# Row maxima issued from ScalarE's queue, group pair sums on GpSimd, and gate products in front of the first maxima

## The reference

```python
q = (q_input @ Wq.T + bq).reshape(B, T, N_HEADS, HEAD_DIM)   # 16 heads of 16
k = q_input @ Wk.T + bk                                      # one head, shared
v = q_input @ Wv.T + bv
mask = pos[None, :] < pos[:, None]                           # strictly causal
attn = softmax(where(mask, einsum('bhtd,bsd->bhts', q, k) * scale, -1e30))
out = einsum('bhts,bsd->bhtd', attn, v) @ Wo.T + bo
...
scores = sigmoid(xf @ w_router); sfc = scores + corr_bias    # 32 experts
top2, _ = top_k(sfc.reshape(T, 8, 4), 2)
group_scores = top2.sum(-1)                                  # best 4 of 8 groups
combine = top 6 experts of these groups, weighted by scores
eo = (silu(x @ gate_w[e]) * (x @ up_w[e])) @ down_w[e]
result = x + attention + sum(combine * eo) + shared expert (width 352)
```

## Time and profile before

| | us |
|---|---|
| median of 3 runs | 699.68 |
| lowest and highest | 697.82, 701.73 |
| profiled execution, its own time | 701.01 |
| profiled execution, span of the trace | 699.2 |

### The profile page before, as it was taken

How to read it: one execution, slowest core, us unless ns; L and a number is a source line. 1 busy time by engine, 2 the same in 40 slices (tenths; PEclk the granted TensorE clock), 3 DMA queues, 4 the chain that set the end, 5 groups by cost and what they waited for, 6 DMA issues and landing times.

```text
span 699.2 us, 13166 instructions
## 1 busy us (share of the span) xinstructions
PE 598.8 (86%) x4249; PEld 334.7 (48%) x4250; DVE 380.7 (54%) x1156; ACT 290.7 (42%) x649; POOL 305.2 (44%) x258
## 2 busy tenths in 40 slices
PE   5959698895879679878969999999999999999940
PEld 2424243442545345534535555555555555555540
DVE  6516874893554355521116656655666665665436
ACT  3644223433332333344454554554454554454400
POOL 4120212130344644465613566566556556556610
PEclk9979899999898889988999999999999999999975
DMA  9679947499587973258754666666666666666479
GB/s 306 164 144 203 351 170 262 61 272 366 161 256 225 318 254 112 101 171 312 277 184 77 105 114 106 106 109 111 105 108 112 104 110 111 105 108 94 55 270 352
DMA packets 73907, 122.92 MB, mean 176 GB/s; under 512 B 12208, under 2 KB 57456, under 8 KB 73328
## 3 DMA queue, kind: packets, MB, share of 16 engines
q1 hardware_dynamic: 50112, 85.22, 41.2%
q0 software_dynamic: 20736, 29.05, 24.3%
q10 hardware_dynamic: 2992, 7.80, 3.1%
HBM read 61.41 MB, written 62.52 MB: 177 GB/s over the span
## 4 chain that ended last, share of the span: by engine, by line
PE 71%; DVE 10%; issue 7%; DMA 7%; SPq 3%; ACT 1%; another core or an unknown queue 1%; POOL 0%; ACTq 0%; DVEq 0%; POOLq 0%
PE bank L1536 20%; PE bank L1562 13%; PE bank L1473 5%; DVE mx L938 5%; PE bank L1518 4%; PE bank L1410 4%; PE bank L1366 4%; PE bank L1392 4%; PE bank L1551 3%; PE bank L1481 2%; PE bank L1369 2%; PE bank L1339 2%; DMA weights<-q_d 2%; SPq L586 2%; PE bank L1394 2%
## 5 line engine op out<-in xcount | busy, mean ns | idle before, releaser
L1306 POOL DMA_INDIRECT acc_d<-attT,xnT x112 | 176.6, 1577 | 146.9 <-ACT attT L821 114.5
L938 DVE TENSOR_REDUCE mx<-bank 128x1 f32<-128x384 f32 (+7 forms) x154 | 106.0, 710 | 80.2 <-PE bank L1369 70.4
L1536 PE MATMUL bank<-weights,xnT 128*64 x448 | 144.5, 465 | 2.6 <-DVE attT L1102 2.4
L1265 POOL DMA_INDIRECT xg_d<-stage,posu x96 | 92.6, 965 | 111.5 <-PE bank L1410 89.7
L766 ACT ACTIVATE xnT<-bank 128x1024 f32<-128x1024 f32 (+1 forms) x72 | 61.7, 882 | 112.8 <-PE bank L1394 76.4
L1562 PE MATMUL bank<-weights,xnT 88*64 x448 | 106.0, 379 | 0.5 <-issue 0.5
L1536 PEld LDWEIGHTS bank<-weights,xnT 128*64 128x64 f32 x448 | 56.7, 136 | 64.1 <-issue 62.4
L1562 PEld LDWEIGHTS bank<-weights,xnT 88*64 88x64 f32 x448 | 61.1, 136 | 41.8 <-issue 17.2
L1102 DVE COPY attT<-weights 128x704 f32 x56 | 29.5, 527 | 92.0 <-PE bank L1539 83.6
L1539 PE MATMUL bank<-attT,xnT 128*64 128x352 f32 x224 | 78.3, 472 | 0.0
L821 ACT ACTIVATE attT<-bank,xnT 128x256 f32<-128x256 f32 x112 | 53.2, 475 | 54.5 <-PE bank L1565 54.5
(11 more groups left out here) (152 smaller groups left out, 1059.5 us busy)
## 6 DMA issues: line engine op xcount, KB each, us to landing
weights<-in_wts SPq DMA_DIRECT2D x32, 608.0 KB
xg_d<-weights SPq DMA_DIRECT2D x28, 584.0 KB, 9.5
stage<-xg_d SPq DMA_DIRECT2D x56, 146.0 KB
xnT<-xg_d SPq DMA_DIRECT2D x56, 146.0 KB
acc_d<-weights SPq DMA_DIRECT2D x8, 512.0 KB, 9.2
q_d<-weights SPq DMA_DIRECT2D x8, 384.0 KB, 3.4
weights<-q_d SPq DMA_DIRECT2D x12, 256.0 KB, 8.6
weights<-q_d SPq DMA_DIRECT2D x48, 64.0 KB, 7.6
```

The costliest lines, as they stand in the source:

```text
L938: eng.tensor_reduce(mx[:, b % 2, h0:h0 + nh * pair, i].rearrange("p (k h) -> p k h", k=pair), bank[:, k:k + pair, 0:wide].rearrange("p k ( ...
L1265: eng.indirect_dma_start(out=xg_d[:, :], out_offset=bass.IndirectOffsetOnAxis(ap=posu[:, t, k:k + 1], axis=0), in_=stage[:, t % NST, :], i ...
L1306: eng.indirect_dma_start(out=acc_d[a][:, :], out_offset=bass.IndirectOffsetOnAxis(ap=index[:, i % NIX:i % NIX + 1], axis=0), in_=ys[y], in ...
L1536: eng.matmul(bank[0:SR, k, 0:2 * M], xgT[i % 4][:, c, 0:SR], weights[:, bass.ds(expert[i] * WCOL + c * 2 * M, 2 * M)], start=(c == 0), sto ...
```

## The change

- The five first products of batch 1 (gate 0, up 0, gate 1, up 1, gate 2, with two gating multiplications) come ahead of the first maxima; they were spread among them.
- The three transfers of a batch's maxima are issued by ScalarE, in a step of their own (`max_out`), no longer by SyncE in `mrows`.
- Maxima and clamp of batches 1 to 3 end at place 36 of 48, `mrows` comes at 38, `max_out` at 40. The rest of the routing is a stream of its own, over places 1 to 42 of batch 0.
- At the end of the opening, gate 0 and up 0 of batch 3 stand between `clamp` and `mrows`.
- The bias and the six pair sums go to POOL (`group_pairs`), into six buffers; VectorE takes the maximum of the six in one reduction (`group_max`).
- Scatters are split 2/5, 2/5 and 1/5 over batches 1 to 3 (they were 3/8, 3/8 and 1/4), the last part ends at place 28, no longer at 34; the first rows are loaded two places earlier.

```diff
-    early = proj_steps((2, KC), (3, KC)) + [("values", 2), ("values", 3), ("sigmoid",)] + gate_steps(1)[:3]
-    later = gate_steps(1)[3:] + proj_steps((2, 0), (2, 1)) + gate_steps(2) + proj_steps((3, 0), (3, 1))
+    steps += gate_steps(1)[:7]
+    early = proj_steps((2, KC), (3, KC)) + [("values", 2), ("values", 3), ("sigmoid",)]
+    later = gate_steps(1)[7:] + proj_steps((2, 0), (2, 1)) + gate_steps(2) + proj_steps((3, 0), (3, 1))
...
-    steps += [("clamp", 0), ("mrows", 0)] + gate_steps(3) + [("warm",)]
+    last = gate_steps(3)
+    steps += [("clamp", 0)] + last[:2] + [last[3], ("mrows", 0), last[2], ("max_out", 0)] + last[4:] + [("warm",)]
...
-    third = len(sends) * 3 // 8
+    third = len(sends) * 2 // 5
...
-        [(0, 40, merged(max_steps(1), routing[EARLY_ROUTING:]) + [("clamp", 1), ("mrows", 1)]),
+        [(0, 36, max_steps(1) + [("clamp", 1)]), (37, 38, [("mrows", 1)]), (39, 40, [("max_out", 1)]), (1, 42, routing[EARLY_ROUTING:]),
...
-        [(14, 26, [("down", 2, i) for i in range(IT)]), (0, 34, sends[2 * third:]), (1, 2, load_steps(*DIES[1])),
+        [(14, 26, [("down", 2, i) for i in range(IT)]), (0, 28, sends[2 * third:]), (1, 2, load_steps(*DIES[1])),
...
+            def group_pairs(n):
+                if n == 0:
+                    w.wait_ge(sigmoid_done, 1)
+                    w.wait_ge(proj_in, 16)
+                    w.wait_ge(pool_ready, 6)
+                    own.mark(eng.tensor_tensor(sfc[:, :, 0:E], scores, cb_sb.unsqueeze(1).to_broadcast([P, NT, E]), ALU.add))
+                    w.wait_ge(pool_step, own.n)
+                for i, (a, c) in enumerate((((0, 1), (0, 2)), ((0, 3), (1, 2)), ((1, 3), (2, 3)))[n]):
+                    eng.tensor_tensor(pairs[:, 2 * n + i], grp[:, :, :, a], grp[:, :, :, c], ALU.add).then_inc(pairs_ready, 1)
...
-                elif kind == "groups":
-                    group_scores(*a)
+                elif kind == "group_max":
+                    w.wait_ge(pairs_ready, 6)
+                    own.mark(eng.tensor_reduce(gsum[:, :, 0:G], pairs.rearrange("p k t g -> p t g k"), AX, ALU.max))
```

More of the change, by code:

```diff
@@ L64 @@
 NPAD = 4
-EARLY_ROUTING, EARLY_CLEARS = 9, 18
+EARLY_ROUTING, EARLY_CLEARS = 10, 18
 CLEARED = (NSLOT + NPAD - 1) // NPAD
@@ L241, in make_plan @@
                         [("zero", n) for n in range(2 * ZEROED)]))],
-        [(0, 40, max_steps(2) + [("clamp", 2), ("mrows", 2)]), (14, 46, [("down", 0, i) for i in range(IT)]),
-         (2, 48, sends[:third]), (8, 48, load_steps(0, DIES[0][0]))],
-        [(0, 40, max_steps(3) + [("clamp", 3), ("mrows", 3)]), (14, 40, [("down", 1, i) for i in range(IT)]),
+        [(0, 36, max_steps(2) + [("clamp", 2)]), (37, 38, [("mrows", 2)]), (39, 40, [("max_out", 2)]), (14, 46, [("down", 0, i) for i in range(IT)]),
+         (3, 48, sends[:third]), (8, 48, load_steps(0, DIES[0][0]))],
@@ L245, in make_plan @@
+        [(0, 36, max_steps(3) + [("clamp", 3)]), (37, 38, [("mrows", 3)]), (39, 40, [("max_out", 3)]), (14, 40, [("down", 1, i) for i in range(IT)]),
          (0, 48, sends[third:2 * third]), (43, 44, load_steps(*DIES[0]))],
-        [(14, 26, [("down", 2, i) for i in range(IT)]), (0, 34, sends[2 * third:]), (1, 2, load_steps(*DIES[1])),
+        [(14, 26, [("down", 2, i) for i in range(IT)]), (0, 28, sends[2 * third:]), (1, 2, load_steps(*DIES[1])),
          (14, 15, load_steps(*DIES[2])), (27, 28, load_steps(*DIES[3])), (35, 36, load_steps(*DIES[4])),
-         (16, 17, [("spread",)]), (20, 21, [("experts",)]), (40, 41, [("first_rows",)]), (46, 47, load_steps(*DIES[5]))],
+         (16, 17, [("spread",)]), (20, 21, [("experts",)]), (38, 39, [("first_rows",)]), (46, 47, load_steps(*DIES[5]))],
@@ L378, in build @@
         sfc = carve([NT, E + 2])
-        pairs = carve([2, NT, G])
+        pairs = carve([6, NT, G])
         gsum = carve([NT, G + 4])
@@ L587, in stack @@
                                   q_d[b, QP[r]].rearrange("(d h) t -> d h t", h=NH)[:, heads, :]).then_inc(stacked[b][g], 16)
-            def max_rows(b):
-                w.wait_ge(mpart_done, b + 1)
-                for j in range(3):
-                    eng.dma_start(qs[b % 2][96 + j:97 + j, :, :].rearrange("p h (i t) -> p (h i) t", t=P),
-                                  mpart[0:NH * IT, b % 2, j, :]).then_inc(max_in[b % 2], 16)
             def clear(n):
@@ L651, in sync_program @@
                     stack(*a)
-                elif kind == "mrows":
-                    max_rows(*a)
                 elif kind == "clear":
@@ L780, in turned_heads, with max_rows @@
                          bank[:, k, :].rearrange("p (i c t) -> p i c t", i=2, c=KC)).then_inc(emptied[k], 1)
+            def max_rows(b):
+                w.wait_ge(mpart_done, b + 1)
+                for j in range(3):
+                    eng.dma_start(qs[b % 2][96 + j:97 + j, :, :].rearrange("p h (i t) -> p (h i) t", t=P),
+                                  mpart[0:NH * IT, b % 2, j, :]).then_inc(max_in[b % 2], 16)
             def gate(b, c):
@@ L853, in scalar_program @@
                     gate(*a)
+                elif kind == "max_out":
+                    max_rows(*a)
                 elif kind == "sa":
@@ L978, in heads @@
                                   ALU.mult).then_inc(emptied[k], 1)
-            def group_scores(n):
-                if n == 0:
-                    w.wait_ge(sigmoid_done, 1)
-                    w.wait_ge(pool_ready, 5)
-                    own.mark(eng.tensor_tensor(sfc[:, :, 0:E], scores, cb_sb.unsqueeze(1).to_broadcast([P, NT, E]), ALU.add))
-                for a, c in (((0, 1), (0, 2)), ((0, 3), (1, 2)), ((1, 3), (2, 3)))[n]:
-                    dst = gsum[:, :, 0:G] if (a, c) == (0, 1) else pairs[:, 0]
-                    w.wait_ge(dve_step, own.n)
-                    own.mark(eng.tensor_tensor(dst, grp[:, :, :, a], grp[:, :, :, c], ALU.add))
-                    if (a, c) != (0, 1):
-                        w.wait_ge(dve_step, own.n)
-                        own.mark(eng.tensor_tensor(gsum[:, :, 0:G], gsum[:, :, 0:G], pairs[:, 0], ALU.max))
             def top(src, dst, done, quarter):
@@ L1280, in gpsimd_program @@
                     split_low(*a)
+                elif kind == "groups":
+                    group_pairs(*a)
                 elif kind == "rmask":
```

8 lines of the change are left out of this document (4 added, 4 removed).

## The result

| | before | after |
|---|---|---|
| median, us | 700.7 | 681.64 (4 runs) |
| lowest and highest, us | 697.82, 701.88 | 678.0, 683.76 |
| ratio to before, 95% interval | | 0.9728 [0.9671, 0.9786] |
| profiled execution, its own time / span | 701.01 / 699.2 | 683.21 / 681.1 |

The changed kernel is 19 us faster. The forecast said 29.3 us faster. The time lies inside the range, near its upper end, and 11 us above the point. In a later group of runs the same kernel came to 0.9664 [0.9610, 0.9719] of the kernel before, 24 us. The question for the experiments is therefore where 5 to 10 us of the forecast went.

A forecast was written before the change was run, and what follows sets the result against it. TensorE (PE), busy 86% of the span, was taken as the bound; only the start of the expert rounds could move. 18 + 4 + 5 + 2.3 + 0 = 29.3 us off the 699.68 median gave 670.4 us, range 660 to 683.

The forecast's parts named there:

- 8.7 + 3.0 - 1.4: Opening: five products leave the maxima stretch (8.7 us), half clock becomes full (3.0), maxima start 1.4 us later.
- two rivals: Opening stays DVE's: 679.4 us, chance 0.2. Maxima land no earlier at two boundaries: 681.7 us, chance 0.14.
- 12.3 us of 18: Whole opening, up to batch 0's first scores: forecast gain 18 us, bounds 9 and 21.7.
- the rival: Opening stays DVE's: reduction waits for POOL, engines alternate badly, gain 9 us instead of 18; 679.4 us, chance 0.2.
- the group sums: Opening: sums moved to POOL remove PE's two idle gaps of 1.77 and 3.75 us, gain 5.5 us.
- this sign of my "I am wrong if": Opening: the forecast is wrong if DVE waits for POOL in front of its new reduction.
- 12.5 us for the end of the opening: Last maxima to first scores of batch 0: 12.5 us (10.8 to 12.9) instead of 15.8, gain 3.3 us.
- gains of 4 and 5 at the boundaries: Maxima issued earlier, from ACT: gain 4 us (3.6 to 4.6) at batches 0 to 1, 5 (4 to 6) at 1 to 2.
- The sign I had named, issue to use above 8 us: Transfers of the row maxima: the forecast is wrong if issue to use exceeds 8 us.
- my rival for the two boundaries: Batches 0 to 1 and 1 to 2: transfer waits in full DMA engines, 9 and 2.3 us given back; 681.7 us, chance 0.14.
- the clock behind the short waits: Behind the first two batch boundaries: short gaps remove half of each slow stretch (2.05 us each), 2.3 us for both.
- sends and first rows at nothing: Batches 1 to 3: new split of sends and earlier first rows cost nothing either way; nothing at 365.5 us waits for them.

The follow-up runs named there:

- the kernel with the hold: Changed kernel, but SyncE waits at batch 0's transfer until ScalarE's maxima have landed: 678.2 us, 0.9601 of the kernel before; repeated on another chip: 650.9 us, 0.9452.
- the third chip: Chip of the third group of experiments; the kernel before took 689.5 us on it.
- the second execution: The changed kernel, unchanged, measured again in the second group: 683.55 us, 0.9664 of the kernel before.
- the second chip: Chip of the second group of experiments; the kernel before took 707.6 us on it.
- the third group: The kernel with the hold again (650.9 us) and three edits to it: hold in every batch 652.38, maxima ending at place 40 652.61, old sends 658.25 us.
- end at place 40: The kernel with the hold, but maxima of batches 1 to 3 end at place 40, not 36, transfer directly behind their transpose: 652.61 us, 0.9462.
- the first chip: Chip of the first group of experiments; the kernel before took 703.9 us on it.
- the second group: Changed kernel again (683.55 us) and edits to it: batch 0's transfer on SyncE 682.69, the kernel with the hold 678.2, old order ending the opening 689.55 us.

## Why the prediction was right or wrong

**Right: the products, their clock, and the maxima stage as a whole.** Gain 12 us alone (8 to 16) against 8.7 + 3.0 - 1.4 = 10.3. The stage took 44.3 us against 43.9.

**The range: in part luck.** The time lies 1.4 us inside its upper end, which I had set by two rivals. Neither of them is what happened. Up to the first scores of batch 0 the change brought 12.3 us of 18, in batches 0 and 1 it brought 5.5 of 10.2, each between the forecast and its rival. And what the opening lacked stood at its end and in its late start, not in the maxima, where the rival had it.

**Partly right: the group sums.** The two gaps went. The wait for POOL, which I took at 0 with 3 us as its other end, was 0 in this profile, but in nine of eleven executions with the sums on POOL VectorE did wait, 2.7 to 4.1 us. The row of the kernel with the hold on the third chip:

```profile
73.63 1.50 DVE L1130 TENSOR_REDUCE weights<-weights 128x128 f32<-128x768 f32 x1 [3.07 <-POOL weights L1229]
```

PE stands still for 1.97 us behind it, so the other end was the commoner one. By that, this sign of my "I am wrong if" came true, at a price of 2 us. The reduction took 1.5 us, not the 1.0 of my sum.

**Wrong in size: the landing of the maxima, and in the opening also the date of its issue.** The step was "from first issue to use took 4.9 us with calm queues and 7.0 with crowded ones", hence 12.5 us for the end of the opening and gains of 4 and 5 at the boundaries. Both bounds came from rows in which SyncE was the issuer. There its own bulk transfers stand behind the maxima. Issued from ScalarE they run beside that bulk and took 8.4 us (8.0 in the second execution) in the opening, 7.5 and 8.9 at the boundaries. The sign I had named, issue to use above 8 us, came true.

At the end of the opening my sum has 5.9 us from the last maxima to the first issue and 6.6 for the landing. Measured were 8.1 and 8.4. So of the 4.0 us too much, 1.8 are the landing, and some 2 lie ahead of the issue, where PE ran at half clock and the transpose waited for a gating multiplication. In the second execution, at full clock, it was 6.5 and 8.0 us, and with the hold 6.5 and 4.9, 1 us less than I had forecast for both together.

At the first boundary the ten executions with ScalarE as the issuer took 7.3 to 9.2 us from issue to use, the four with SyncE 5.2 to 7.0. The DMA engines were busy all the time in the first kind (a share of 1.05 from 153.7 to 161.2 in the changed kernel) and for 0.82 of it in the kernel before, from 168.4 to 175.4, where the prediction calls them full. At the second boundary the issuer makes no visible difference: 6.6 to 9.1 us with ScalarE, 6.9 to 8.3 with SyncE. So crowding by SyncE's own queue is shown for the opening and fits the first boundary; for the second it isn't shown.

The Trainium skill (page "DMA: Bandwidth & Descriptors", section "Issuing engines are not separate DMA queues") says that another issuing engine saves only the time of issuing, and stood behind my rival for the two boundaries. These runs say it holds for the transfer and not for the wait ahead of it: a second issuer removed some 4 us in SyncE's queue (batch 0 took 51.8 instead of 55.6 us), and it didn't keep the bulk away from the transfer.

**Wrong: the clock behind the short waits.** I credited 2.3 us if the gaps became short. They became short (1.88 and 1.52 us), and PE still ran at 0.61 and 0.52 behind them; in the opening the new gap of 3.35 us brought a new stretch at 0.51 (107.6 to 111), worth some 1.7 us in batch 0, and the wait of 1.39 us at 90.30 another (columns as in the earlier trace rows):

```profile
90.30:94.00 3.70, 3.70 (x8) 1.70 (x9) 3.53 (x15) 0.29 (x1) 3.54 (x5) 0.54 0.51 205
```

In every run the boundary from batch 0 to 1 was followed by such a stretch, 4.1 us at 0.50 to 0.71. At the next boundary the second execution of the changed kernel and the kernel with the hold on the second chip kept 1.00; neither waited for the maxima there. The two kernels of the third group behind the boundary from batch 1 to 2, with the new and with the old sends (busy PE, clock, DMA share and GB/s):

```profile
209.80:213.90 4.10, 4.07 (x35) 0.69 1.03 321
213.20:217.30 4.10, 4.05 (x23) 0.50 0.92 356
```

Their waits were 2.53 and 4.34 us. But the length of the wait alone doesn't give the clock: behind 2.41 us (end at place 40) it was 0.50, behind 8.81 us (the sums alone) 0.58. A wait of 1.39 us was followed by 0.54 in one execution of the changed kernel and by 1.00 in the other, and 2.94 us in the opening left 1.00 where 3.35 us didn't. So no run gives the rule that I assumed. From 0.50 to 0.6 or 0.7 is worth 0.4 to 0.8 us at each boundary, not the 1.15 that I took.

**Wrong on the third chip, open on the first: sends and first rows at nothing.** I looked only at the date of the first expert product, which a weight load set, and not at the first rows ahead of it. In the trace of the kernel before nothing waited for them, as the missing bracket shows:

```profile
361.10 0.66 PE L1518 MATMUL bank<-first_sb,stage 128*128 128x128 f32 x4
```

The changed kernel has no wait there either, in both executions. The wait appeared on the third chip, where the batches before are shorter, and the part is worth some 6 us there. The old sends were not tried elsewhere. If they cost anything on the first chip too, this error is in the change's favour, and the losses elsewhere are larger than the 11 us between forecast and result.

**Right: the expert rounds.** They are as long as before: from the first expert product to the end of the span it is 333.4 us, against 333.7 (PE busy 292.16 of the first 292.5 us, against 292.01 in the earlier trace rows). They began at 347.7, not 336. On the third chip, where the kernel with the hold began them at 312.5, it is 336.2 us; so an earlier start isn't handed on in full.

**What stays open: batches 1 to 3.** From the first scores of batch 1 to the first expert product the kernel before took 190.1 us; the changed kernel 186.5 (188.6 in its second execution), where I had 182.8. The kernel with the hold, one and the same program, took 187.5 us in the second group and 159.6 in the third. First the second group, batches 1, 2 and 3, then the third (the second row of the second group begins 1.5 us ahead of the first scores of batch 2, at 215.86):

```profile
152.10:214.40 62.30, 54.94 (x441) 31.08 (x441) 33.40 (x66) 22.57 (x29) 29.08 (x30) 0.95 0.82 257
214.40:281.00 66.60, 57.88 (x458) 31.67 (x459) 33.42 (x66) 24.78 (x32) 36.81 (x39) 0.92 0.53 175
281.00:339.60 58.60, 47.72 (x349) 25.18 (x347) 6.62 (x21) 27.11 (x37) 26.53 (x28) 0.88 0.74 254
```

```profile
152.90:209.80 56.90, 53.50 (x449) 31.25 (x449) 33.17 (x66) 23.93 (x30) 31.77 (x33) 0.97 0.91 288
209.80:264.90 55.10, 53.65 (x450) 30.89 (x451) 33.22 (x66) 23.82 (x30) 34.84 (x37) 0.97 0.61 208
264.90:312.50 47.60, 41.15 (x346) 22.92 (x346) 6.59 (x21) 26.27 (x37) 25.92 (x27) 0.98 0.92 312
```

PE's idle time is 27.0 us in the one and 11.3 in the other, and its busy time 160.5 and 148.3 because of the clock. The waits of POOL in that stretch (total, times, longest) show what kind of idle it is; "remote" is a wait that ended with nothing the profile knows:

```profile
POOL xg_d L1270 <- issue: 53.7, 72, 31.6
POOL xg_d L1270 <- PE bank L1417: 32.1, 17, 5.2
POOL xg_d L1270 <- remote: 14.4, 7, 2.4
```

The third chip shows no row "remote" for POOL, and in the kernel with the hold no stop of PE over 1 us in that stretch but those for the maxima and the one at the first expert product. On the second, stops of some 2 us appear on all engines while POOL scatters. ScalarE and PE at one of them:

```profile
214.21 1.51 ACT L765 ACTIVATE xnT<-bank 128x1024 f32<-128x1024 f32 x2 [2.75 <-remote]
215.29 0.64 PE L1417 MATMUL bank<-xnT,v_sb 128*32 128x256 f32 x8 [2.36 <-ACT xnT L765]
```

The changed kernel has the same rows (PE at 226.90 above; POOL "remote" 10.1 us in 5 times), and so has the kernel before in its batches 1 to 3 (POOL 1.4 us in 2 times, ScalarE 14.1 in 6). Since one program has them on one chip and not on the other, they are no part of the change. The kernel before also gains 11 to 18 us on the third chip, the one with the hold 27. So a part of what the change frees seems to be lost again to these stops where they occur. That is argued from the totals; the changed kernel itself wasn't run on the third chip, no trace of the kernel before was taken there, and the cause of the stops isn't known.

## What to carry to other kernels

In this kernel a small transfer moved out of a busy queue lost two things at once: the wait behind the others, and the shelter from the others, which until then could not start before it. Bound its landing by rows in which the bulk runs beside it, and where the bulk can wait, let its queue wait for the landing; here that one wait brought the first scores 3.4 us forward (the totals, 0.9601 and 0.9664 of the kernel before, have intervals that overlap). The wait works only on what stands behind it: in the later batches it changed nothing. And price every part that the diff holds by the first instruction that needs its data, not by the last wait of the stage, and ask whether that data is still in time when the stage gets shorter: the sends that I gave nothing were worth some 6 us on one chip.

## What the runs showed of the hardware

- Three transfers of 16 KB were used 4.9 to 5.2 us after their issue, without a wait, when the bulk stood or was held behind them at the end of the opening, and 8.0 to 8.4 us when it ran beside them. At the first boundary it was 5.2 to 7.0 us with SyncE and 7.3 to 9.2 with ScalarE as the issuer.
- Issuing three transfers kept ScalarE's queue busy for 1.8 to 3.4 us, and where they stood between exponentials the next one came 0.8 to 3.1 us late.
- PE ran 3.7 us at 0.54 behind a wait of 1.39 us in one execution of the changed kernel and at 1.00 behind the same wait in another.
- One program took 678.2 us on one chip and 650.9 on another. The difference stood almost wholly in the stretch of 190 us in which POOL scatters and the DMA engines are busy 0.53 to 0.92 of the time; the opening began its first scores at 100.14 and 100.63.
